# A ring of gathered rows with 10 buffers in place of 24

## The chip, the cores and the metric

The kernel runs on one core of one Trainium2 chip. The metric is the device time of one execution in microseconds (us). One core has TensorE (PE), VectorE (DVE), ScalarE (ACT), GpSimd (POOL) and SyncE (SP), and 16 DMA engines that they share. DMAs are issued here by SP, ACT and POOL; POOL issues the gathers.

## What is computed

The tower of a recommendation model, for a batch of 512 samples: 32 embedding rows of 256 numbers per sample, the dot products of all pairs of them, and three dense layers.

```python
def reference(dense_ctx, ids, tbl_0, ..., tbl_31, W_top1, b_top1, W_top2, b_top2, W_top3):
    e = jnp.stack([tbl_0[ids[:, 0]], ..., tbl_31[ids[:, 31]]], axis=1)   # 512 x 32 x 256
    iu, ju = jnp.triu_indices(32, k=1)
    z = jnp.einsum('bnd,bmd->bnm', e, e)[:, iu, ju]                      # 512 x 496
    h = jnp.concatenate([z, dense_ctx], axis=1)                          # 512 x 512
    h = jnp.maximum(h @ W_top1 + b_top1, 0.0)
    h = jnp.maximum(h @ W_top2 + b_top2, 0.0)
    return h @ W_top3                                                    # 512 x 1
```

Everything is float32. Ten tables have 12500 rows; the others have 1000 or 1250.

## The kernel before

**Tiles.** The batch is cut into 4 blocks of 128 samples, and each block into 32 groups of 4 samples (a group is 4 x 32 = 128 embedding rows, one per partition). The unit of loading is a *fetch*: 128 rows of 1 KB, 128 KB in all. There are 118 fetches, taken two at a time: 59 *pairs*, pair p being fetches 2p and 2p + 1. Blocks 1 to 3 need fewer than 32 fetches because up to four small tables are "hot": these are loaded whole (`hot_sb`, 1 MB each, in two halves issued by ACT), and PE looks their rows up by a matmul with a 0/1 mask (`look_up`, L457; ten units of 16 steps, spread over pairs 1 to 38).

**How rows come in.** 115 of the 118 fetches are gathered by POOL, each by one indirect DMA into a buffer of the ring `rows` (L204), in the order of the fetches. Buffer n % `RING` has a semaphore of its own, `rows_landed` (L279), for which PE waits before the transposes. The other three fetches, 43, 83 and 109 (`SINGLE`, L75), are brought row by row, 1 KB a DMA: 320 rows by SP in one long sequence (L377), 64 by ACT. They have buffers of their own, so they don't touch the ring.

**How POOL is held back.** The whole of POOL's loop is this:

```python
393  for n, fetch in enumerate(GATHERED):
394      if n == RING:
395          pool.wait_ge(idx_ready, 2)
396      if n >= RING:
398          pool.wait_ge(transposed, GATHERED[n - RING] + 1)
399      pool.indirect_dma_start(rows[:, n % RING, :], None, tables, ...).then_inc(rows_landed[n % RING], 16)
```

Gather n waits until PE has transposed the fetch that used the buffer before. `transposed` counts fetches (L419); it is signalled by the second transpose of each fetch, and POOL, DVE and ACT all wait for it.

**What a pair costs PE** (the loop at L605 to L612): the transposes of its two fetches (L417, 128x128 float32 through the identity, two per fetch), then the dot products of the pair before (`gram_pair`, L448: small matmuls into `gram_ps`, L432), then some steps of a look-up (L468), and in later pairs a piece of the dense layers for a block that is complete (`mlp_at`: h1 at L498, h2 at L575, y at L587) or, for the last block, for 32 samples at a time (`set_at`, L517 to L555). `gram_pair` needs DVE's copy of the transposes from PSUM to SBUF (`copy_pair`, L680: L334 in block 0, L345 and L337 later), and that copy waits for `transposed`. Before the loop PE runs 26 and 36 passes through the identity (L476) that only keep it busy, with fetches 0 and 1 between them. Pair 58 and the last 32 samples come after the loop.

**Order around the change.** PE, DVE and ACT go by pair, with tables of what is done at which pair (`DOTS_AT`, `MLP_AT`, `LOOKUP_AT`, `LOAD_AT`, `SETS_AT`). ACT's loads of the hot tables and weights also wait for `transposed`, so they follow PE. Only SP's row copies go by their own clock. DVE adds table starts to indices in two parts, of which the first is the part that the first ring of gathers needs (L653: columns 0 to `RING`, then the rest).

Of the kernel before, what the change touches and what calls it, by code (L numbers as in the profile page):

```python
# [46 lines left out]
FIRST_FETCH = tuple(sum(BLOCK_FETCHES[:b]) for b in range(BLOCKS))  # L47
FETCHES = sum(BLOCK_FETCHES)
PAIRS = FETCHES // 2
RING = 24  # L50

PARTS = tuple((BLOCK_GROUPS * b + first, BLOCK_GROUPS * b + end) for b in range(BLOCKS)
              for first, end in (((0, 16), (16, 32)) if b < BLOCKS - 2 else
# [132 lines left out]
def tower_kernel(nc, ids, single_ids, hot_ids, hot_tables, tables, dense, w1, w1_packed, w2, vectors, tail, y):  # L186
    with ExitStack() as ctx:
        def sb(name, shape, dt=F32):
            return ctx.enter_context(nc.sbuf_tensor(name, shape, dt))
# [4 lines left out]
        def sem(name):  # L194
            return ctx.enter_context(nc.semaphore(name))
# [3 lines left out]
        ident = sb("ident", [P, P])  # L199
        rows = sb("rows", [P, RING, DIM])  # L200
        single_sb = sb("single_sb", [1, 2, SP_ROWS + ACT_ROWS], I32)
# [76 lines left out]
        hot_copied = sem("hot_copied")  # L278
        rows_landed = [sem(f"rows_landed_{n}") for n in range(RING)]  # L279
        single_landed = [sem(f"single_landed_{n}") for n in range(len(SINGLE))]  # L280
# [103 lines left out]
        def _(pool):  # L384
# [8 lines left out]
            for n, fetch in enumerate(GATHERED):  # L393
                if n == RING:
                    pool.wait_ge(idx_ready, 2)
                if n >= RING:

                    pool.wait_ge(transposed, GATHERED[n - RING] + 1)
                pool.indirect_dma_start(rows[:, n % RING, :], None, tables,  # L399
                                        bass.IndirectOffsetOnAxis(idx[:, fetch:fetch + 1], 0)  # L400
# [612 lines left out]
```

## Time and profile before

| | us |
|---|---|
| median of 3 runs | 240.64 |
| lowest, highest | 239.93, 241.45 |
| the profiled execution | 239.78 |
| its span, first to last instruction | 237.4 |
| PE busy, share of the span | 169.8, 72% |
| POOL busy, share of the span | 110.3, 46% |
| mean granted clock of PE | 0.892 of full speed |

The profiled execution's time is 2.4 us more than its span, for what lies before the first and after the last instruction. Times in rows are us from the start of the span unless marked ns. In rows with an engine name, "PEld" is the load of a matmul's stationary operand and "SPq" or "ACTq" an issue of a DMA. "<-remote" and "<-issue" in brackets mean that the profile shows no instruction that ended the wait. The page's slices cut the span into 40 parts of 5.9 us.

### The profile page before, as it was taken

How to read it: one execution, taken by the hardware profiler on the slowest of the kernel's cores; microseconds unless marked ns; L12 is line 12 of the kernel's file. 1: busy time of each engine (PE TensorE's matmuls, PEld its weight loads, DVE VectorE, ACT ScalarE, POOL GpSimd, SP SyncE). 2: the span in 40 equal slices, each digit the busy share in tenths (PEclk: the TensorE clock that was granted, in tenths of full speed). 3: DMA queues.
4: the chain of work that ended last, by engine and by line, in shares of the span. 5: the costliest groups of instructions: out<-in, count | busy, mean ns of one | idle time of the engine just before them, and what ended most of it. 6: DMA issues, size and time to landing. Idle time of an engine off the chain costs nothing.

```text
span 237.4 us, 8126 instructions
## 1 busy us (share of the span) xinstructions
PE 169.8 (72%) x3274; PEld 145.1 (61%) x3274; DVE 94.6 (40%) x308; ACT 51.0 (21%) x162; POOL 110.3 (46%) x122
## 2 busy tenths in 40 slices
PE   7821103978777777594877859969768688899976
PEld 7710002867666566583756748859646467798764
DVE  2600001214443526254254521742346417556572
ACT  0000001010132011412104320332024334425360
POOL 5777772556555565464354461556455614000000
PEclk9985555899999999769999995998999959999999
DMA  2763331557756543623235452423232312000000
GB/s 86 242 232 111 110 98 44 174 137 250 246 142 185 155 136 78 206 68 83 75 114 160 138 160 74 139 77 95 74 89 71 91 44 74 11 3 3 6 3 3
DMA packets 11349, 25.44 MB, mean 107 GB/s; under 512 B 2943, under 2 KB 4559, under 8 KB 11313
## 3 DMA queue, kind: packets, MB, share of 16 engines
q0 software_dynamic: 5520, 15.08, 21.2%
q10 hardware_dynamic: 5004, 9.40, 13.3%
q1 hardware_dynamic: 788, 0.45, 0.7%
q8 instruction: 25, 0.41, 0.7%
q14 instruction: 12, 0.09, 0.2%
HBM read 24.70 MB, written 0.00 MB: 104 GB/s over the span
## 4 chain that ended last, share of the span: by engine, by line
PE 46%; issue 20%; another core or an unknown queue 15%; DVE 6%; ACTq 6%; ACT 3%; DMA 2%; POOL 1%
PE hot_ps L468 12%; PE gram_ps L432 12%; PE xt_ps L417 7%; PE act_ps L498 4%; ACTq L366 4%; PE dve_ps L498 3%; DVE z L325 2%; DVE xt L337 2%; PE hot_ps L476 2%; PE dve_ps L575 2%; PE hot_ps L517 2%; PE act_ps L575 1%; ACT z L318 1%; ACTq L811 1%
## 5 line engine op out<-in xcount | busy, mean ns | idle before, releaser
L399 POOL DMA_INDIRECT rows<-tables,idx x115 | 109.5, 952 | 88.5 <-PE xt_ps L417 46.1
L432 PE MATMUL gram_ps<-xt 128*32 128x32 f32 x1888 | 46.3, 205 | 45.4 <-issue 44.1
L432 PEld LDWEIGHTS gram_ps<-xt 128*32 128x32 f32 x1888 | 33.3, 113 | 62.6 <-issue 59.9
L468 PE MATMUL hot_ps<-mask,hot_sb 128*128 128x128 f32 x320 | 50.7, 308 | 10.3 <-ACT hot_xt L848 6.4
L468 PEld LDWEIGHTS hot_ps<-mask,hot_sb 128*128 128x128 f32 x320 | 43.1, 210 | 12.3 <-issue 11.0
L417 PE MATMUL xt_ps<-ident,rows 128*128 128x128 f32 x228 | 38.1, 289 | 2.2 <-issue 1.4
L334 DVE COPY xt<-xt_ps 128x512 f32<-128x512 f32 x16 | 11.1, 692 | 60.4 <-remote 32.7
L345 DVE COPY last_xt<-xt_ps 128x64 f32<-128x64 f32 (+3 forms) x44 | 10.8, 245 | 58.8 <-PE xt_ps L417 42.8
L417 PEld LDWEIGHTS xt_ps<-ident,rows 128*128 128x128 f32 x228 | 28.6, 150 | 4.0 <-issue 2.4
L351 ACT COPY xt<-hot_xt 128x64 f32<-128x64 f32 (+1 forms) x43 | 10.2, 236 | 91.8 <-remote 63.2
L337 DVE COPY xt<-xt_ps 128x448 f32<-128x448 f32 (+2 forms) x43 | 26.7, 620 | 0.0
L318 ACT COPY z<-gram_ps 32x128 f32<-32x128 f32 (+1 forms) x56 | 19.4, 346 | 9.4 <-remote 8.1
L318 DVE COPY z<-gram_ps 32x128 f32<-32x128 f32 (+1 forms) x56 | 19.1, 342 | 0.9
L675 DVE TENSOR_SCALAR mask<-hot_ids_sb,hot_number 128x128 f32<-128x128 int32 x80 | 17.4, 311 | 0.0
L848 ACT COPY hot_xt<-hot_ps 128x256 f32<-128x256 f32 x10 | 6.1, 611 | 30.1 <-remote 16.0
L476 PE MATMUL hot_ps<-ident 128*128 128x128 f32 x62 | 9.0, 316 | 1.6 <-POOL ident L389 1.6
L848 ACT ACT_TABLE_LOAD x1 | 1.3, 1283 | 40.7 <-remote 40.7
L476 PEld LDWEIGHTS hot_ps<-ident 128*128 128x128 f32 x62 | 8.7, 167 | 1.6 <-POOL ident L389 1.6
L325 DVE COPY z<-gram_ps 32x64 f32<-32x64 f32 (+1 forms) x32 | 8.4, 263 | 1.2 <-PE gram_ps L432 0.8
L325 ACT COPY z<-gram_ps 32x64 f32<-32x64 f32 (+1 forms) x32 | 8.5, 267 | 1.6 <-PE gram_ps L432 1.1
L498 PE MATMUL act_ps<-z,w_packed_sb 128*128 128x128 f32 x48 | 8.9, 329 | 0.0
L498 PE MATMUL dve_ps<-z,w_packed_sb 128*128 128x128 f32 x48 | 7.9, 291 | 0.4 <-issue 0.2
(71 smaller groups left out, 89.6 us busy)
## 6 DMA issues: line engine op xcount, KB each, us to landing
single_rows<-tables SPq DMA_DIRECT2D x320, 1.0 KB
hot_sb<-hot_tables ACTq DMA_DIRECT2D x8, 512.0 KB
w_sb<-w ACTq DMA_DIRECT2D x8, 256.0 KB
rows<-tables,idx POOLq DMA_INDIRECT x115
w_packed_sb<-w_packed ACTq DMA_DIRECT2D x5, 256.0 KB
single_rows<-tables ACTq DMA_DIRECT2D x64, 1.0 KB
hot_ids_sb<-hot_ids ACTq DMA_DIRECT2D x3, 256.0 KB, 3.1
w_sb<-w ACTq DMA_DIRECT2D x1, 512.0 KB
```

Of the source, the lines that this page charges most:

```text
L318: last = copy(z_by_quad[FIELDS * jq:FIELDS * (jq + 1), q, first:end, :].rearrange("p g (h s) -> p g h s", s=FOURS), gram_ps[FIELDS * q:FIE ...
L325: last = copy(z_by_quad[FIELDS * jq:FIELDS * (jq + 1), q, first:end, lo:SLOTS], gram_ps[FIELDS * q:FIELDS * (q + 1), part % 3, 0:end - fir ...
L334: return copy(xt[:, bank, :, places].rearrange("p k l q f -> p (k l q f)"), xt_ps[:, bank, :, places].rearrange("p k l r -> p (k l r)"))
L337: return copy(xt[:, bank, :, places].rearrange("p k l q f -> p (k l) q f")[:, :, :, 0:COLD[b]], xt_ps[:, bank, :, places, 0:OWN[b]].rearra ...
L345: return copy(to[:, :, :, field:field + count].rearrange("p k s f -> p k f s"), ps)
L399: pool.indirect_dma_start(rows[:, n % RING, :], None, tables, bass.IndirectOffsetOnAxis(idx[:, fetch:fetch + 1], 0)).then_inc(rows_landed[ ...
L417: last = nc.tensor.transpose(xt_ps[:, fetch // 2 % 2, k, fetch % 2, :], x[:, P * k:P * (k + 1)], ident[:])
L432: last = nc.tensor.matmul(gram_ps[FIELDS * q:FIELDS * (q + 1), part % 3, at, :], x, x, start=(k == 0), stop=(k == CHUNKS - 1))
L468: last = nc.tensor.matmul(hot_ps[:, k, :], hot_sb[:, l, c, P * k:P * (k + 1)], mask[:, unit % MASKS, c, :], start=(c == 0), stop=(c == HOT ...
L476: nc.tensor.transpose(hot_ps[:, 0, :], ident[:], ident[:])
L498: last = nc.tensor.matmul(h1_ps[m], w1_packed_sb[:, s, P * m:P * (m + 1)], z[:, FOURS + s, samples] if s < FOURS else z_alone[:, samples], ...
L675: last = nc.vector.tensor_scalar(mask[:, unit % MASKS, c, :], hot_ids_sb[:, b, l, :], hot_number[:, c:c + 1], None, ALU.is_equal)
```

## The change

```diff
@@ -47,7 +47,7 @@
 FIRST_FETCH = tuple(sum(BLOCK_FETCHES[:b]) for b in range(BLOCKS))
 FETCHES = sum(BLOCK_FETCHES)
 PAIRS = FETCHES // 2
-RING = 24
+RING = 10
```

`RING` is used in five places: the size of `rows` (L204), the number of `rows_landed` semaphores (L279), POOL's loop (L393 to L401), PE's wait (L410 to L412), and the split of DVE's index sum (L653). A gather now waits for the transposes of the fetch that stands 10 gathers before it, where it was 24. What is gathered, computed and stored is the same, and so is the order of each engine's instructions.

## Rows read from the trace of the kernel before

**Rows 1.** The page: busy times; 40 slices of POOL and of PE's clock

```profile
PE 169.8 (72%) x3274; PEld 145.1 (61%) x3274; DVE 94.6 (40%) x308; ACT 51.0 (21%) x162; POOL 110.3 (46%) x122
...
POOL 5777772556555565464354461556455614000000
PEclk9985555899999999769999995998999959999999
```

**Rows 2.** Stretches: length, busy us of each engine (instructions), clock, DMA share, GB/s

```profile
12.00:18.00 6.00, 1.56 (x13) 0.89 (x12) 0.23 (x1) 0.00 (x0) 4.48 (x6) 0.81 0.68 226
18.00:24.00 6.00, 0.63 (x3) 0.38 (x3) 0.00 (x0) 0.00 (x0) 4.48 (x6) 0.50 0.35 105
...
42.00:48.00 6.00, 5.55 (x96) 4.96 (x96) 1.38 (x2) 0.01 (x1) 3.50 (x4) 0.91 0.50 157
```

**Rows 3.** Timeline of POOL: start, us, instruction [idle before it]

```profile
3.31 1.31 POOL L399 DMA_INDIRECT rows<-tables,idx  x1 [1.73 <-DVE idx L654]
...
17.50 0.94 POOL L399 DMA_INDIRECT rows<-tables,idx  x1 [0.30 <-issue]
...
34.98 0.95 POOL L399 DMA_INDIRECT rows<-tables,idx  x1 [0.30 <-issue]
40.47 0.95 POOL L399 DMA_INDIRECT rows<-tables,idx  x1 [4.55 <-remote]
...
46.99 0.94 POOL L399 DMA_INDIRECT rows<-tables,idx  x1 [1.03 <-PE xt_ps L417]
...
50.36 0.94 POOL L399 DMA_INDIRECT rows<-tables,idx  x1 [1.17 <-PE xt_ps L417]
...
53.66 0.94 POOL L399 DMA_INDIRECT rows<-tables,idx  x1 [1.11 <-PE xt_ps L417]
```

**Rows 4.** Timeline of PE, first 44 us

```profile
13.30 0.44 PE L417 MATMUL xt_ps<-ident,rows 128*128 128x128 f32 x2 [0.99 <-issue]
...
37.31 0.21 PE L432 MATMUL gram_ps<-xt 128*32 128x32 f32 x1 [2.59 <-issue]
...
40.12 0.46 PE L432 MATMUL gram_ps<-xt 128*32 128x32 f32 x14 [0.50 <-issue]
...
43.48 0.46 PE L432 MATMUL gram_ps<-xt 128*32 128x32 f32 x32
```

**Rows 5.** Timeline of DVE: the copies of pairs 1, 4, 5 and 6

```profile
40.28 0.69 DVE L334 COPY xt<-xt_ps 128x512 f32<-128x512 f32 x1 [28.05 <-remote]
...
50.17 0.69 DVE L334 COPY xt<-xt_ps 128x512 f32<-128x512 f32 x1 [2.68 <-PE xt_ps L417]
53.47 0.69 DVE L334 COPY xt<-xt_ps 128x512 f32<-128x512 f32 x1 [2.61 <-PE xt_ps L417]
...
56.81 0.69 DVE L334 COPY xt<-xt_ps 128x512 f32<-128x512 f32 x1 [1.08 <-PE xt_ps L417]
```

**Rows 6.** Timeline of SP, from three windows: 0 to 20, 20 to 40, 40.2 to 84

```profile
6.20 12.88 SPq L366 DMA_DIRECT2D single_rows<-tables  x17
...
20.47 18.90 SPq L366 DMA_DIRECT2D single_rows<-tables  x9
...
40.11 42.30 SPq L366 DMA_DIRECT2D single_rows<-tables  x101
```

**Rows 7.** Timeline of POOL: its last gather

```profile
198.62 0.95 POOL L399 DMA_INDIRECT rows<-tables,idx  x1 [0.30 <-issue]
```

**Rows 8.** Timeline of DVE: the first copy of pair 53

```profile
215.65 0.21 DVE L345 COPY last_xt<-xt_ps 128x32 f32<-128x32 f32 x1 [1.05 <-PE xt_ps L417]
```

**Rows 9.** Timeline of PE at pair 48: the second part of y

```profile
204.28 0.38 PE L587 MATMUL dve_ps<-h,vec_sb 128*1 128x128 f32 x2 [0.60 <-ACT h L883]
```

**Rows 10.** The stretch from 43 to 97 us, columns as in rows 2

```profile
43.00:97.00 54.00, 41.85 (x763) 35.46 (x761) 21.69 (x62) 6.58 (x17) 30.61 (x33) 1.00 0.57 171
```

**Rows 11.** The chain that ended last, near its start: start, us, what

```profile
4.92 2.75 DMA rows<-tables,idx
```

**Rows 12.** Timeline of PE: the transposes of fetch 43

```profile
106.26 0.38 PE L417 MATMUL xt_ps<-ident,single_rows 128*128 128x128 f32 x2
```

## The prediction

> **What bounds the kernel now.** I read the page's slices first, then a table of stretches, then the timelines of POOL, PE and DVE. TensorE is busy 72% of the span, so it looks like the bound, but the slices say where it is not: its granted clock is 0.5 of full speed (1.2 instead of 2.4 GHz) in slices 4 to 7, while POOL is busy 5 to 7 tenths there [rows 1]. The table by stretch makes that sharp: from 18 to 24 us PE works 0.63 of 6 us at a clock of 0.50, and from 42 to 48 us it works 5.55 of 6 [rows 2]. So about 26 us at the start are nearly lost.
>
> What holds it? POOL's timeline [rows 3]: the gathers start at 3.31 and follow each other every 1.25 us without a wait, up to the one that starts at 34.98. That is 26 of them: 24 buffers, and two more because fetches 0 and 1 were transposed early. The 27th waits for `transposed` to count fetch 2, and it starts only at 40.47, after 4.55 us of waiting. But PE ran the transposes of fetch 3 at 13.30 [rows 4]. DVE, which waits for the same count, starts its copy at 40.28 after 28.05 us of idling [rows 5]. So the work was done and its semaphore seems to be seen 27 us later. In between PE's small matmuls trickle (37.31 after a gap of 2.59), although they depend on nothing unfinished. SP, which has nothing to do with them, issues 17 row copies up to 19 us, 9 in the next 19, and 101 in the 42 us after 40.11 [rows 6]. Every engine crawls while gathers are queued back to back, and all are free together at about 40.1.
>
> Is it the number of gathers? The steady part answers. There POOL issues two per pair: it starts at 46.99, 50.36 and 53.66 [rows 3], and DVE's copies of the next pair start at 50.17, 53.47 and 56.81 [rows 5]. From the first gather of a burst of two to the release is 3.18, 3.11, 3.15 us, mean 3.15. From the first gather of the burst of 26 to the release is 40.28 - 3.31 = 36.97 us. A line through both: (36.97 - 3.15) / 24 = 1.41 us per gather, and 0.33 us beside. I take this as the working model: **signals come through when the burst is worked off, 0.33 + 1.41 N us after its first gather**. The issue rate of POOL (1.25 us) is a little faster than that, so a backlog grows. The same model gives the pace of the steady part: a pair takes 3.34 us (46.99 to 50.36 to 53.66), though PE has less to do. What the resource is that the gathers fill, no row says.
>
> **The change part by part.** Nothing is computed differently. `RING` sets four things.
>
> 1. *The first burst.* With 10 buffers, POOL goes 12 gathers far (10, and two by fetches 0 and 1, which are counted at 8 us), and then waits for fetch 2. Up to the twelfth, which starts at 17.50 [rows 3], all is as before. By the model the release comes 0.33 + 12 x 1.41 = 17.2 us after 3.31, at 20.5 instead of 40.28: **-19.7 us**. From both sides: the last gather ends at 18.44; the shortest drain seen is about 1.0 us (a burst of two from 46.99 ends at 49.19, release 50.17), the longest 4.35 (34.98 + 0.95 to 40.28). So the release lies between 19.4 and 22.8, a gain of 17.5 to 20.9. I take the line, since 12 lies between its two points. PE will have more of the small matmuls of pair 0 still to do when it is let go: some 10 to 15 at 14 to 33 ns (32 in 0.46 us at the full clock, 14 in 0.46 just after the release, [rows 4]), +0.3 us, bound 0 to 0.5.
>
> 2. *The late gathers.* The 14 gathers that are no longer in the first burst are not gone: POOL is 7 pairs further behind all the time. Before, the last gather starts at 198.62 [rows 7], after the transposes of pair 46, and pairs 47 to 53 run without gathers: DVE's copy for pair 53 starts at 215.65 [rows 8], 17.03 us for 7 pairs, 2.43 each. Now gathers go on until pair 53, and these seven pairs take the pace of gathers: 7 x 3.34 = 23.4, which is +6.3. One of the pairs has a wait of its own, 0.60 us for the ReLU of h2 before y [rows 9]; I add 0.4 to 0.5 for that, an estimate, since it may come on top of the pace: **+6.8 us**. From below: 7 x 3.15 = 22.0, +5.0. From above, if a gather costs its 1.41 us on top of PE's work: 7 x (2.43 + 2.82) = 36.8, +19.7. I take the value near the low end, because the row of the steady part is the nearest: from 43 to 97 us PE is busy 41.85 us [rows 10] over some 16 pairs, 2.6 each, with two gathers in each, and a pair takes 3.34, not 2.6 + 2.8 = 5.4. Gathers and PE's work overlap.
>
> 3. *The lead.* A buffer is now filled 5 pairs ahead of its use, not 12. Five pairs are 5 x 3.34 = 16.7 us; of that the signal and two gathers take 3.15. That leaves 13.5 us for landing. The second gather landed 2.75 us after its start [rows 11]. At the worst, beside 1.5 MB of hot tables, the fourth (by POOL's pace it starts near 7.4) was used at 13.30 [rows 4], 5.9 us. Both fit; cost 0. If that cover were gone, each us over 13.5 would cost one us in five pairs, 9 us in the whole. One rule speaks against the change: the Trainium skill, "DMA: Bandwidth & Descriptors", Rules for kernel authors, says to issue a DMA early and wait for it late. By the fit of the same page of the Trainium skill (Anatomy of one DMA — SWDGE (gpsimd) path: a fixed 2.0 us, and the bytes at 436 GB/s) a gather of 128 KB takes 2.3 us, an estimate; the trace has 2.75. By either figure the lead is enough, and the rule would give 0 here.
>
> 4. *Things on their own clock.* SP brings the rows of fetch 43 one by one, and PE needs them at 106.26 [rows 12], which becomes 86.5. By the counts of [rows 6] the 127th copy is issued at about 82. Now 17 are out by 20.5 and 111 follow at 42.30 / 101 = 0.42 us: done at 67. The hot tables are loaded at PE's pace, so they move along. The split of the index sum moves from column 25 to 11, before the first gather: nothing. Cost 0.
>
> Sum: -19.7 + 6.8 + 0.3 = -12.6. The profiled execution took 239.78 us (span 237.4), so 227.2 us (span about 224.8). It lies 0.86 below the median of 240.64; the median of the changed kernel should be 240.64 - 12.6 = **228.0 us**.
>
> **The rivals.**
> *A, gathers are only moved (same).* Each gather costs its 1.41 us wherever it stands, so what 14 of them cost at the start comes back at the end: -19.7 + 19.7 + 0.3, 240.9 us. For it: POOL's total is the same, and POOL and the late pairs must share. Against it: the steady part, as above. 8%.
> *B, the release at 40 has another cause (slower).* Something on its own schedule (the copies of SP, PE's instructions) ends the crawl at 40.1, whatever POOL does. Then only the late part is left: 240.64 + 6.8 = 247.4 us. It decides if DVE's copy for pair 1 stays at 40. For it: the crawl goes on 4 us after POOL's last gather. Against it: SP goes on with its copies after 40.11 at more than twice the rate, so it isn't their number, and the line explains the 4 us. 8%.
> *C, ten buffers starve PE.* Place: the wait for `rows_landed` before the transposes. It decides where landing exceeds 13.5 us; at 15 us throughout it would take back the 13 us, and the kernel would be at 241. Nothing landed slower than 5.9. 4%. This is also what the rule of the Trainium skill's page on DMA (above) would mean, if it decided here; so far the trace doesn't bear it out.
> *D, in between:* the release is later than the line says, or the late pairs take 4 us and more, since PE's own waits there add to those of the signals: 232 to 238 us. 10%.
>
> **How the numbers follow.** The forecast has 70%. Its own bounds: -20.9 + 5.0 = -15.9 gives 224.7, and -17.5 + 0.5 + 9.3 (seven pairs at 3.76) gives 232.9. I set the range at 224.0 to 234.0, which takes in the forecast and a part of D; A, B and C lie outside it. About 1% (2.4 us) is what a measurement of this kernel can tell from no change. Faster by over 1%: the forecast and D, and a little of A and C, 0.82. Within 1%: most of A and part of C, 0.09. Slower: B and the rest, 0.09.
>
> **What would show it.** Right: POOL has 12 gathers back to back and then a first wait that ends near 20.7; DVE's second copy starts at about 20.5; the clock falls to 0.50 only for a slice or two; the steady pairs keep 3.34 us; the last gather starts after the transposes of pair 53, near 203; from pair 54 on all is as before, 12.6 us earlier; PE has no wait on a gather's landing beyond the first ones. Wrong: a release at 40 (B); late pairs above 5 us (A); waits of PE for DMA rows in the middle (C). The forecast as a whole fails if the release is right but the steady pairs become longer than 3.34 us.

## The result and the profile after

| | before | 10 buffers |
|---|---|---|
| median, us | 240.28 (4 runs, 239.31 to 241.45) | 227.23 (4 runs, 226.31 to 228.82) |
| ratio, 95% interval | | 0.9501 (0.9447 to 0.9555) |
| the profiled execution, us | 239.78 | 226.31 |
| its span, us | 237.4 | 223.9 |
| mean granted clock | 0.892 | 0.931 |

The ratios of this document leave out runs that took over 1.5% more than the fastest of their kernel; the medians do not. The forecast was 228.0, with a range of 224 to 234. Of the profile after, the page's busy times and slices answer to [rows 1]:

```profile
PE 172.3 (77%) x3274; PEld 146.3 (65%) x3274; DVE 94.4 (42%) x308; ACT 51.0 (23%) x162; POOL 110.6 (49%) x122
...
POOL 4774565556556555265555355555553556541000
PEclk9995699999999999679996999999796799999999
```

Busy times have hardly changed; the idle time has. The low clock is down to two slices at the start, and POOL is now busy almost to the end. The timeline of POOL, to be held against [rows 3, 7]:

```profile
3.39 1.33 POOL L399 DMA_INDIRECT rows<-tables,idx  x1 [1.81 <-DVE idx L654]
...
17.61 0.94 POOL L399 DMA_INDIRECT rows<-tables,idx  x1 [0.30 <-issue]
21.09 0.94 POOL L399 DMA_INDIRECT rows<-tables,idx  x1 [2.53 <-remote]
...
168.11 0.95 POOL L399 DMA_INDIRECT rows<-tables,idx  x1 [0.94 <-remote]
...
174.81 0.95 POOL L399 DMA_INDIRECT rows<-tables,idx  x1 [4.49 <-PE xt_ps L417]
...
178.01 0.95 POOL L399 DMA_INDIRECT rows<-tables,idx  x1 [1.00 <-PE xt_ps L417]
...
201.95 0.94 POOL L399 DMA_INDIRECT rows<-tables,idx  x1 [2.13 <-PE xt_ps L417]
```

The burst is 12 gathers long, and the 13th waits until 21.09. DVE's copies of pair 1 and of pair 53 answer to [rows 5, 8]:

```profile
20.89 0.69 DVE L334 COPY xt<-xt_ps 128x512 f32<-128x512 f32 x1 [8.55 <-remote]
...
201.94 0.21 DVE L345 COPY last_xt<-xt_ps 128x32 f32<-128x32 f32 x1 [1.37 <-PE xt_ps L417]
```

The copy of pair 1 moves from 40.28 to 20.89 us. SP, whose work the change does not touch, is freed at the same time. Its timeline up to 20.4 us and from there to 64 us, against [rows 6]:

```profile
6.30 14.33 SPq L366 DMA_DIRECT2D single_rows<-tables  x20
...
19.94 44.25 SPq L366 DMA_DIRECT2D single_rows<-tables  x106
```

Where the 13.5 us of span went, from these rows:

| stretch | before | after | change |
|---|---|---|---|
| start to DVE's copy of pair 1 | 40.28 | 20.89 | -19.4 |
| to POOL's start behind pair 46 (198.62; 178.01) | 158.3 | 157.1 | -1.2 |
| to DVE's copy of pair 53 | 17.0 | 23.9 | +6.9 |
| to the end of the span | 21.7 | 22.0 | +0.2 |
| sum | 237.4 | 223.9 | -13.5 |

### The profile page after: what moved, and what is told of

Same layout as the page of the kernel before. It is cut to its first block, busy times and chain, and to the rows that moved or that the text cites. A ratio compares the mean times of both kernels' runs of the same rounds, so it can differ in the third digit from the quotient of the medians.

```text
span 223.9 us, 8126 instructions
## 1 busy us (share of the span) xinstructions
PE 172.3 (77%) x3274; PEld 146.3 (65%) x3274; DVE 94.4 (42%) x308; ACT 51.0 (23%) x162; POOL 110.6 (49%) x122
## 4 chain that ended last, share of the span: by engine, by line
PE 38%; another core or an unknown queue 25%; issue 11%; ACTq 9%; ACT 7%; DVE 5%; DMA 2%; POOL 1%
PE gram_ps L432 9%; PE hot_ps L468 8%; PE xt_ps L417 7%; ACTq L366 5%; PE act_ps L498 4%; ACT z L318 3%; ACTq L811 3%; PE dve_ps L498 3%; PE hot_ps L517 2%; DVE z L325 2%; ACT hot_xt L848 2%; PE hot_ps L476 2%; ACT xt L351 2%; DVE xt L337 2%
## 5 line engine op out<-in xcount | busy, mean ns | idle before, releaser
L432 PE MATMUL gram_ps<-xt 128*32 128x32 f32 x1888 | 47.8, 206 | 29.0 <-issue 27.9
L432 PEld LDWEIGHTS gram_ps<-xt 128*32 128x32 f32 x1888 | 34.6, 113 | 46.3 <-issue 44.2
L468 PE MATMUL hot_ps<-mask,hot_sb 128*128 128x128 f32 x320 | 49.3, 302 | 10.7 <-ACT hot_xt L848 9.1
L468 PEld LDWEIGHTS hot_ps<-mask,hot_sb 128*128 128x128 f32 x320 | 41.9, 205 | 12.7 <-issue 11.5
L417 PE MATMUL xt_ps<-ident,rows 128*128 128x128 f32 x228 | 37.9, 288 | 1.8 <-issue 1.2
L345 DVE COPY last_xt<-xt_ps 128x64 f32<-128x64 f32 (+3 forms) x44 | 10.8, 245 | 57.6 <-PE xt_ps L417 45.0
L417 PEld LDWEIGHTS xt_ps<-ident,rows 128*128 128x128 f32 x228 | 28.4, 149 | 3.6 <-issue 2.6
L334 DVE COPY xt<-xt_ps 128x512 f32<-128x512 f32 x16 | 11.1, 692 | 41.2 <-PE xt_ps L417 24.1
L498 PEld LDWEIGHTS act_ps<-z,w_packed_sb 128*128 128x128 f32 x48 | 7.5, 231 | 0.4 <-issue 0.2
```

Of the source, the lines that this page charges most:

```text
L417: last = nc.tensor.transpose(xt_ps[:, fetch // 2 % 2, k, fetch % 2, :], x[:, P * k:P * (k + 1)], ident[:])
L432: last = nc.tensor.matmul(gram_ps[FIELDS * q:FIELDS * (q + 1), part % 3, at, :], x, x, start=(k == 0), stop=(k == CHUNKS - 1))
L468: last = nc.tensor.matmul(hot_ps[:, k, :], hot_sb[:, l, c, P * k:P * (k + 1)], mask[:, unit % MASKS, c, :], start=(c == 0), stop=(c == HOT ...
L498: last = nc.tensor.matmul(h1_ps[m], w1_packed_sb[:, s, P * m:P * (m + 1)], z[:, FOURS + s, samples] if s < FOURS else z_alone[:, samples], ...
```

## The experiments

The theory going in: a burst of N gathers holds back every engine's signals for 0.33 + 1.41 N us. The rivals: the crawl ends by something else, such as SP's row copies; a gather costs the same wherever it stands; the size of the ring as such matters.

The twelve runs were made on several chips, and this turned out to be the main finding. The kernel before takes 240.3 us on the chip of the result above. On two numbered chips it takes 241.3 us (one run) and 242.5 us (median of seven, 240.2 to 243.6 and one of 248.0), but on two others 164 to 167 us (16 runs). The chip of the result has no number on record, so it may be one of the first two. I call the first kind crawling and the second quiet.

**First set, which met a quiet chip (kernel before: 165.85 us).**

*Distance without the size.* 24 buffers, each gather waiting for the fetch 10 before it:

```diff
+AHEAD = 10
-                if n >= RING:
-                    pool.wait_ge(transposed, GATHERED[n - RING] + 1)
+                if n >= AHEAD:
+                    pool.wait_ge(transposed, GATHERED[n - AHEAD] + 1)
```

> 24 buffers and 24 semaphores, but each gather waits for the fetch that stands 10 gathers before it. Theory (only the length of the first burst and the distance POOL runs ahead matter): 12 gathers, DVE's copy of pair 1 at 20.9 us and the last gather near 202, as with 10 buffers; 227 us. Rival (the size of the ring in memory or the number of its semaphores matters): another time, up to the 240 of before.

Measured: 163.87 us in one run.

*SP later.*

```diff
             sp.wait_ge(row_at_ready, 1)
+            sp.wait_ge(transposed, 4)
```

> 24 buffers as before, and SP starts its single-row copies only when fetch 3 has been transposed and signalled. Theory (the crawl comes from gathers back to back): POOL still has 26 gathers, the release stays at 40.3 us give or take 1, and the time at 240. Rival (SP's copies and the gathers together make the crawl): the release comes early, near 14 us, since fetch 3 is transposed at 13.3, and the time falls by 15 us or more.

Measured: 174.21 us in one run. There was no crawl to explain here. The 8 us are another thing: PE waits 12.8 us in two stretches for rows of SP's fetches, since on a quiet chip PE reaches fetch 43 much sooner. SP's copies as a cause of the crawl were not tried on a crawling chip.

*16 buffers.*

```diff
-RING = 24
+RING = 16
```

> 16 buffers: a burst of 18 gathers. The line of the prediction, checked at a point between: first gather plus 0.33 + 18 x 1.41 = 25.7 us, so DVE's copy of pair 1 at 29.1 us; the late part costs 4 pairs at 0.98 us over before, +3.9 us; 240.3 - 11.2 + 3.9 = 233.0 us. Rival (the crawl has a fixed end or a threshold in the number of gathers): release near 20 or near 40.

Measured: 165.92 us in one run, as the kernel before.

*POOL's first burst spaced out.*

```diff
+        pad = sb("pad", [P, 2 * 26, 32])
...
                                         ).then_inc(rows_landed[n % RING], 16)
+                for m in range(2 if n < 26 else 0):
+                    nc.gpsimd.memset(pad[:, 2 * n + m, :], 0.0)
```

> 24 buffers as before, and after each of the first 26 gathers POOL also clears two scraps of memory, so that it issues slower than it did (the aim is 1.6 us or more instead of 1.25). Theory (a backlog grows since a gather needs 1.41 us of something and POOL issues one per 1.25): with a pace above 1.41 no backlog grows, so the signals of fetch 3 come through soon after 14 us while the burst goes on, and PE starts its pairs 20 us earlier; time below 230 us. Rival (a gather in hand blocks the signals as long as the queue is never idle, whatever the pace): the release comes after the 26th gather, which is now later than 36: 45 us or more, and the time above 245.

Measured: 165.63 us in one run; the clears brought the pace only from 1.25 to 1.31 us, so the edit missed its aim too. None of the four expectations could be tested, because the thing they are about wasn't there. A burst of 18 gathers, and so the line between 12 and 26, was never tried on a crawling chip.

**The quiet chip looked at for itself.** The changed kernel ten times and 6 buffers four times, on another chip (kernel before: 164.61 us, 13 runs):

```diff
-RING = 24
+RING = 10
```

> The changed kernel itself again, beside the kernel before. On a chip where the crawl of the start exists (before near 240 us) it should repeat: 227 us, DVE's copy of pair 1 at 20.9. On a chip without it (before near 166 us, as in the four runs before this one) POOL issues one gather per 1.25 us from the first to the last and sets the end in both kernels; then the theory that the gain is the length of the crawl expects no difference, 164 to 166.5 us. Rival (a shorter ring helps or hurts by itself): more than 1% away from the kernel before.

```diff
-RING = 24
+RING = 6
```

> 6 buffers. With the crawl: a burst of 8, release at 3.4 + 0.33 + 8 x 1.41 = 15.0 us, two more late pairs with gathers (+2.0), so 227.2 - 5.6 + 2.0 = 223.6 us, if the lead of 3 pairs (10.0 us, of which 6.9 for landing) is enough. Without the crawl: POOL is 6 gathers ahead at most, 7.5 us of its own pace; where PE holds a pair for longer than that (the block ends) POOL stops and can't catch up: 2 to 8 us over before. Rival (ring depth is of no account): as before.

Measured: 10 buffers 165.00 us, ratio **1.0005 (0.9963 to 1.0048)**; 6 buffers 169.86 us, ratio 1.0198 (1.0083 to 1.0312). The same edit that gives 5% on one chip gives nothing on another. With 6 buffers the cost of too short a lead does appear. It is that of POOL being stopped: the view of POOL's waits has

```profile
POOL rows L399 <- PE xt_ps L417: 13.8, 29, 3.4
```

(us in all, times, the longest), where 10 buffers have 8.5 us in 28 waits, the longest 0.3. The last gather starts at 153.11 instead of 146.88.

One of the four runs with 6 buffers, on this same quiet chip, took 257.03 us, with a granted clock of 1.0, beside 170.39, 169.34 and 167.99. The ratio leaves it out, the median doesn't, and there is no trace of it. So which chip it is does not decide alone: a single execution on a quiet chip can be as long as one on a crawling chip. Whether that was the same crawl is not known.

Then the kernel before once more, unchanged, to have its trace:

> The kernel before, unchanged, to have its trace from another execution. If the crawl is a matter of the chip or of the execution and not of the kernel, the trace shows none here: about 165 us, DVE's copy of pair 1 at about 13.8, and POOL issuing every 1.25 us from its first gather to its last with waits of 0.3 us only. If the crawl belongs to the kernel: 240 us and the copy at 40.

Measured: 165.68 us. Its POOL slices, DVE's copy of pair 1, and the summary of the gathers (releasers of POOL's waits, and time to landing):

```profile
POOL 3777777777777777777777777777777777772000
```

```profile
13.91 0.69 DVE L334 COPY xt<-xt_ps 128x512 f32<-128x512 f32 x1 [1.59 <-PE xt_ps L417]
```

```profile
L399 POOL DMA_INDIRECT rows<-tables,idx x115: 945/949/1314, 3.4 to 147.4; - x115
its engine sat idle before it (us, times) until:
  issue: 27.5, 90
  PE xt_ps L417: 7.3, 24
  DVE idx L654: 1.8, 1
...
DMA to landing us min/median/max: 2.7/3.6/5.8
```

The copy of pair 1 starts at 13.91, right after the transposes, although POOL sends gathers back to back as in [rows 3]. POOL is never held: 7.3 us in 24 waits is 0.3 us each, its own step from one gather to the next. It issues from 3.4 to 147.4 us at 1.26 us each, and the rest of the span is the tail. A depth of 10 instead of 24 changes nothing as long as POOL is not stopped. With 10 buffers its last gather starts at 146.88:

```profile
146.88 0.95 POOL L399 DMA_INDIRECT rows<-tables,idx  x1 [0.30 <-PE xt_ps L417]
```

SP's row copies show the difference best. The registers' MOVE and the DMA issue of one row, in the crawling profile of the kernel before and in the quiet one (min/median/max in ns):

```profile
L366 SPq MOVE single_rows<-tables x320: 2/29/702, 6.1 to 163.7; - x160
L366 SPq DMA_DIRECT2D single_rows<-tables x320: 2/228/715, 6.2 to 163.8; - x160
```

```profile
L366 SPq MOVE single_rows<-tables x320: 29/29/42, 6.2 to 133.8; - x160
L366 SPq DMA_DIRECT2D single_rows<-tables x320: 221/228/502, 6.3 to 133.9; - x160
```

A MOVE takes 29 ns at the median in both; in the crawling profile it takes up to 702. The profile shows no wait at it, and nothing in the program ties it to the gathers. That speaks against a dependency; what holds it is not shown.

**Is POOL's pace the bound on a quiet chip?** Six one-column clears behind every gather:

```diff
+        pad = sb("pad", [P, 690])
...
                                         ).then_inc(rows_landed[n % RING], 16)
+                for m in range(6 if n < 115 else 0):
+                    nc.gpsimd.memset(pad[:, 6 * n + m:6 * n + m + 1], 0.0)
```

> 24 buffers, and six one-column clears after every one of the 115 gathers, which should bring POOL's pace from 1.25 to about 1.55 us. With the crawl (before near 240): a pace slower than 1.41 us lets the signals through, the release comes before 20 us and the time is below 215. Without the crawl: if POOL's pace sets the end, 115 x 0.30 = 34 us more, 199 us; if PE sets it, at most 175 us.

Measured: 175.40 us in one run (kernel before 166.54). The last rows of POOL in a window up to 162 us:

```profile
157.07 0.96 POOL L400 DMA_INDIRECT rows<-tables,idx  x1
158.03 0.26 POOL L404 MEMSET pad<- 128x1 f32 x6
158.44 0.95 POOL L400 DMA_INDIRECT rows<-tables,idx  x1 [0.15 <-issue]
```

The pace became 1.37 us, not 1.55, so the last gather starts at 158.44, 11.0 us later than 147.4, and the span grew by 9.7 (163.3 to 173.0). The expectation's 34 us are wrong because the clears hide in POOL's step between gathers, but per us of pace the answer is clear: nearly all of POOL's delay, 9.7 of 11.0 us, reaches the end. PE's waits for gathered rows grow from 9.1 us in 13 waits to 17.1 in 16. So a slower POOL makes the kernel longer there. That a faster POOL would make it shorter is not shown: PE is busy 89% of the span of 161.5 us in the run with the distance of 10.

**Second set, crawling chips.** Twelve clears after each of the first 26 gathers (kernel before: 241.30 us):

```diff
+        pad = sb("pad", [P, 312])
...
+                for m in range(12 if n < 26 else 0):
+                    nc.gpsimd.memset(pad[:, 12 * n + m:12 * n + m + 1], 0.0)
```

> 24 buffers, and twelve one-column clears after each of the first 26 gathers only, which should bring POOL's pace there to about 1.7 us (six made 1.36 of 1.25). With the crawl (before near 240): a pace well above 1.41 us leaves no backlog, the signals of fetch 3 come before 20 us and the time is below 225; rival (any burst holds the signals to its end): release at 49, time above 247. Without the crawl (before near 165): POOL is 26 x 0.45 = 12 us late after the first burst and has no slack to make it up, so if POOL's pace sets the end the time is 177; rival (PE sets the end and POOL's lead covers it): at most 168.

Measured: 246.19 us in one run. DVE's copies of pairs 1 to 5:

```profile
16.19 0.69 DVE L335 COPY xt<-xt_ps 128x512 f32<-128x512 f32 x1 [3.61 <-PE xt_ps L420]
26.45 0.69 DVE L335 COPY xt<-xt_ps 128x512 f32<-128x512 f32 x1 [9.56 <-remote]
35.18 0.69 DVE L335 COPY xt<-xt_ps 128x512 f32<-128x512 f32 x1 [8.04 <-remote]
45.48 0.69 DVE L335 COPY xt<-xt_ps 128x512 f32<-128x512 f32 x1 [9.61 <-remote]
56.67 0.69 DVE L335 COPY xt<-xt_ps 128x512 f32<-128x512 f32 x1 [10.50 <-PE xt_ps L420]
```

Neither answer as written. The first release comes at 16.19, which excludes the rival (held to the end of the burst): with POOL's pace at 1.5 to 1.7 us signals come through inside the burst. But the theory failed too. With every gather further from the last than 1.41 us no backlog should be left, and yet only one pair gets through in 9 to 11 us. So 1.41 us per gather fits the end of an unbroken burst and does not describe what happens inside one. The 312 clears may add to the load; nothing here separates them from the gathers. The early pairs were no gain: POOL then makes up its arrears in a burst without clears.

```profile
44.79 0.95 POOL L400 DMA_INDIRECT rows<-tables,idx  x1 [0.15 <-remote]
...
53.55 0.95 POOL L400 DMA_INDIRECT rows<-tables,idx  x1 [0.30 <-issue]
56.86 0.94 POOL L400 DMA_INDIRECT rows<-tables,idx  x1 [2.37 <-PE xt_ps L420]
```

From 44.79 to 53.55 are 8 gathers, and the release is at 56.67: 11.88 us. The line gives 0.33 + 8 x 1.41 = 11.6.

Then three more on another chip (kernel before: 242.46 us, 7 runs). With 8 buffers:

```diff
-RING = 24
+RING = 8
```

> 8 buffers. With the crawl (before near 240): a burst of 10 gathers, release at 3.4 + 0.33 + 10 x 1.41 = 17.8 us, one more late pair with gathers (+1.0), 227.2 - 2.8 + 1.0 = 225.4 us. Without it (before near 165): between 10 buffers (same as before) and 6 (2.0% over before): 0 to 1.5% over.

With 4 buffers:

```diff
-RING = 24
+RING = 4
```

> 4 buffers, a lead of 2 pairs. With the crawl: a burst of 6, release when fetches 2 and 3 have landed and are transposed, 14 us instead of 20.9 with 10 buffers; but the lead is 6.7 us, of which 3.5 are left for landing, less than the 5.9 us a gather takes beside the hot tables: PE waits for rows in the first 50 us; 225 to 240. Without the crawl: POOL has to wait for PE at nearly every pair and each gather's landing (3.6 us) is on the path: over 15% slower than before, 190 us or more.

With a distance that grows:

> 24 buffers; POOL runs 10 gathers ahead at first and is let 8 further ahead in the pairs in which it stood idle for longer (two more from pair 22, one from 26, two from 30, three from 44). With the crawl: the release stays at 20.9 us and four of the seven late pairs lose their gathers, -3.9 us, of which the long pairs take back 1 to 2: 224 to 226 us, against 227.2 with 10 buffers. Rival (a gather costs the same wherever it stands): 227. Without the crawl: as before, within 1%.

This last one keeps 24 buffers and lets the distance grow:

```diff
+AHEAD = ((0, 10), (22, 12), (26, 13), (30, 15), (44, 18))
...
+def fetch_before(n):
+    for fetch in range(FETCHES):
+        ahead = max(a for pair, a in AHEAD if fetch // 2 >= pair)
+        if sum(g <= fetch for g in GATHERED) + ahead > n:
+            return fetch
...
-                if n >= RING:
-                    pool.wait_ge(transposed, GATHERED[n - RING] + 1)
+                if n >= AHEAD[0][1]:
+                    pool.wait_ge(transposed, fetch_before(n) + 1)
```

| | us, median of 4 | ratio, 95% interval |
|---|---|---|
| 8 buffers | 228.94 | 0.9453 (0.9343 to 0.9562) |
| 4 buffers | 227.71 | 0.9368 (0.9259 to 0.9478) |
| distance 10, growing to 18 | 236.54 | 0.9786 (0.97 to 0.9871) |

The time with 8 buffers is 3.5 us over its expectation, of which 2.2 are in the kernel before on this chip as well. The time with 4 buffers lies in its range, and the growing distance missed both of its answers.

DVE's copy of pair 1 with 8 buffers, with 4, and with the growing distance:

```profile
17.98 0.69 DVE L334 COPY xt<-xt_ps 128x512 f32<-128x512 f32 x1 [5.91 <-remote]
```

```profile
13.95 0.69 DVE L334 COPY xt<-xt_ps 128x512 f32<-128x512 f32 x1 [1.78 <-issue]
```

```profile
20.73 0.69 DVE L343 COPY xt<-xt_ps 128x512 f32<-128x512 f32 x1 [8.71 <-remote]
```

With these the line can be checked at lengths between its two points (time from the burst's first gather to the release):

| gathers in the burst | measured | 0.33 + 1.41 N |
|---|---|---|
| 6 (4 buffers) | 10.6 | 8.8; fetch 3 is only just transposed |
| 8 (behind the spaced burst) | 11.9 | 11.6 |
| 10 (8 buffers) | 14.7 | 14.4 |
| 12 (10 buffers; growing distance) | 17.5; 17.5 | 17.3 |
| 26 (before) | 37.0 | 37.0, by construction |

It holds for the unbroken bursts of 8, 10 and 12 gathers, and for rings of different size; the growing distance, with 24 buffers and a burst of 12, has the release of 10 buffers. So the size of the ring as such is out, and so is a fixed end of the crawl (rival B). With 4 buffers the first release is held no more (13.95 against 13.91 on the quiet chip); most later pairs still take 3.3 to 3.5 us, as with 10 buffers. But now PE waits for landings, 5.9 us in 8 waits:

```profile
PE xt_ps L417 <- DMA rows<-tables,idx: 5.9, 8, 1.4
```

The intervals of 4, 8 and 10 buffers overlap, so which is best on a crawling chip is not settled, only that the last steps are small.

The growing distance is the instructive failure. It was to put 8 gathers into pairs in which POOL stands idle for longer, and so to free the late pairs. It is 3% slower than 8 buffers on the same chip. The pair from 168.11 to 174.81 in the profile of 10 buffers (above) has two gathers and 6.70 us. With five gathers it is:

```profile
176.99 0.94 POOL L408 DMA_INDIRECT rows<-tables,idx  x1 [1.03 <-remote]
...
187.84 0.94 POOL L408 DMA_INDIRECT rows<-tables,idx  x1 [4.91 <-PE xt_ps L426]
```

10.85 us, 4.15 more for three gathers, 1.38 each. All four places lie between DVE's copies of pair 22 and of pair 45. With 10 buffers, and with the growing distance, these two start at:

```profile
89.11 0.27 DVE L345 COPY last_xt<-xt_ps 128x64 f32<-128x64 f32 x1 [1.14 <-PE xt_ps L417]
...
175.00 0.22 DVE L345 COPY last_xt<-xt_ps 128x32 f32<-128x32 f32 x1 [5.03 <-PE xt_ps L417]
```

```profile
91.16 0.27 DVE L354 COPY last_xt<-xt_ps 128x64 f32<-128x64 f32 x1 [1.20 <-PE xt_ps L426]
...
188.03 0.22 DVE L354 COPY last_xt<-xt_ps 128x32 f32<-128x32 f32 x1 [9.20 <-PE xt_ps L426]
```

That is 85.9 us and 96.9, 11.0 more for 8 gathers, 1.4 each. Against 8 buffers on the same chip (88.2 us) it is 8.7, 1.1 each. A single place tells less: from DVE's copy of pair 29 to that of pair 31 it takes 13.7 us with two gathers more, but without them 10.8, 9.7 and 10.3 in the kernel before, with 10 and with 8 buffers. The late pairs gave back some 4 us. So POOL's idle time was no room. I read it like this, and no run separates it further: the steps of such a pair wait for each other by signals, which are held until the gathers are worked off, and only then does the pair's own work go on. Only the first place, four gathers from 91.35 with the next at 97.62, took hardly more (6.27) than with two (89.30 to 95.34, 6.04).

No run beat the changed kernel beyond its interval on a crawling chip. On the quiet chip 6 buffers cost 2%; 4 and 8 were not tried on one.

## Why the prediction was right

Step by step, for the chip on which it was measured:

1. *The first burst.* Said: release at 20.5, -19.7 us. Measured: 20.89, -19.4. The line rested on two lengths and holds to 0.3 us at three more (8, 10 and 12 gathers); at 6 the transposes come later than it. Between 12 and 26 nothing was measured. The line is a description: the run with twelve clears shows that the backlog behind it, a gather needing 1.41 us and coming every 1.25, is not the whole mechanism.
2. *The late gathers.* Said: seven pairs from 17.03 to 23.4 us, and 0.4 beside, +6.8. Measured: 23.9 us, +6.9. The value near the low end was right: gathers and PE's work overlap in part, and 14 gathers cost 0.5 us each. That the sum came out so closely is partly luck, since the seven pairs did not take one common pace of 3.34 us. By the distances between DVE's copies pairs 47 to 53 took 2.8, 3.6, 4.1, 2.4, 3.0, 3.4 and 4.6 us, and before 1.5, 2.7, 3.3, 2.2, 2.1, 2.1 and 2.8: long pairs grew too, by up to 1.8. In the long pairs of the growing distance a gather costs 1.1 to 1.4 us. Rival A was wrong for this edit and near the truth for that one.
3. *The lead.* Said: 13.5 us for a landing that takes 5.9 at worst, cost 0. With 10 buffers PE waits for gathered rows once, 0.6 us, and with 8 twice, 1.1 us in all. The quiet profile gives the landing directly, 5.8 us at most. What the rule in the Trainium skill, "DMA: Bandwidth & Descriptors", Rules for kernel authors, warns of (issue early, wait late) shows at 6 buffers on the quiet chip (+2.0%) and in the waits with 4 on the crawling one; at 10 it gives 0, as said.
4. *Other clocks.* Said: SP's 128 rows out by 67, needed at 86.5. Measured: 20 + 106 = 126 copies are out by 64.2 us, the 128th by 65.6. Cost 0.
5. *PE's remainder.* Said: +0.3 us behind the release, for 10 to 15 more small matmuls. DVE's copy of pair 2 starts 3.73 us after that of pair 1, where it was 3.37: +0.4, of which pair 3 gives back 0.2. But it was 6 more matmuls (20 where there were 14), and the transposes of pair 2 took 1.06 us instead of 0.73, so the size is about right and the reason for it only in part.
6. *Not foreseen:* -1.2 us in the middle. By the distances between DVE's copies it stands at three places: pair 19 takes 1.3 us less than before, pair 23 takes 1.3 more, pairs 30 and 31 take 1.1 less. I have no row that names a cause, and it may be the spread of single executions.

The sum was -12.6; the medians differ by -13.05, the spans by -13.5.

What the prediction left out is greater than any of its errors. It took the crawl for a property of the kernel. It said that "what the resource is that the gathers fill, no row says", and gave no rival in which that resource has another size elsewhere. On the quiet chip where both kernels ran the forecast fails: the ratio is 1.0005, and the range would not have held the time.

## What to carry to other kernels

When engines that share nothing in the program slow down together, and a plain register MOVE takes 0.7 us, suspect something that all of them pass through, and fit the delay against the length of the burst before it: two lengths gave a line here that held at three others. A ring is a lead and a burst at once. Its depth needs to cover the landing time (3.6 us typical, 5.8 at most here) and the longest pair, in which a short ring stops POOL (3.4 us with 6 buffers). Here 10 buffers cover both, and on a crawling chip more depth only lets the burst grow. An idle engine is not room for more work before it is known what the others wait for in that time. And measure the kernel before on more than one chip before believing that a gain, or an idle engine, belongs to the kernel.

## What the runs showed of the hardware that was not expected

- The same program takes 164 to 167 us on two chips and 239 to 248 on the others, in every run made there of the kernel before. PE's and DVE's instructions take nearly the same time each (a transpose at L417 289 and 281 ns in the mean, DVE's copy at L334 692 and 692, crawling and quiet); what differs is when signals are seen and how fast sequencers step.
- Without gathers a crawling chip is as fast as a quiet one. From DVE's copy of pair 49 to that of pair 58 the kernel before takes 20.47 us on the crawling chip, where POOL's gathers are over, and 20.50 on the quiet chip. So the crawl goes with the gathers in flight, and not with the work of PE and DVE as such.
- In the crawling profiles many waits have no recorded releaser ("remote"), in the quiet one of the kernel before none of POOL's or DVE's has. The views of waits, crawling and quiet:

```profile
POOL rows L399 <- PE xt_ps L417: 46.1, 31, 5.1
...
DVE xt L334 <- remote: 32.7, 4, 28.0
...
POOL rows L399 <- remote: 19.1, 14, 4.5
```

```profile
POOL rows L399 <- issue: 27.5, 90, 0.3
...
DVE xt L334 <- PE xt_ps L417: 21.3, 15, 3.7
...
POOL rows L399 <- PE xt_ps L417: 7.3, 24, 0.3
```

- So records of signals go missing where signals are late. The six crawling traces hold 1158 to 1329 records of semaphore updates by DMAs, the eight quiet ones 2876 to 2992; of updates by engines they hold 731 to 750 and 771 to 779. In the kernel before, no update by an engine is recorded from 20 to 40 us, where the quiet trace has 49. The Trainium skill, "NOTIFIC — the notification-queue block", section 7.1, says that the block which writes such records can hold back its producers when it can't pass them on. That would fit the delay, on a chip with a slower way out for records, and would mean that the crawl comes with the recording; that records are also lost would need something more. No run here shows it: every run has the profiler's span and clock, so none tells how the kernel does without the recording, and the cause of the crawl stays open.
- By the fit a gather holds the signals for 1.41 us on a crawling chip, with POOL issuing one per 1.25; slowing POOL to about 1.6 us let signals through, one pair in 9 to 11 us, where 3.3 us is the pace with two gathers a pair.
- Small clears behind a gather are nearly free on POOL: six of them added 0.11 us to its pace, not 0.3, since they run in the 0.30 us that it takes from one gather to the next.
